# One tower layer of a vision transformer on one core: maxima and exponentials of the next head group issued ahead of the inversion and the splitting of the present one

## The chip, the cores and the metric

The kernel runs on one core of a Trainium2 chip. The metric is the time of one execution on the device in microseconds (us), the median over runs. Five engines run their own instruction streams in order and meet only at semaphores: TensorE (PE, with its weight loads as PEld), VectorE (DVE), ScalarE (ACT), GpSimd (POOL) and SyncE (SP), which here issues every DMA.

## The reference, cut to what matters

For 64 blocks of 128 tokens by 1024 features (the blocks are the filters that a state-space kernel generator makes of the input x), a layer of attention and then one of a feed-forward matrix with low-rank experts are computed:

```python
h = tok(log_dt, x, B, inv_A_real, A_imag, 1024)          # [64, 128, 1024]
h = h + attn(layernorm(h), wq, wk, wv, wo)               # 32 heads of 32, 8 key heads, rotary, causal softmax
h = h + ffn(layernorm(h), W_base, b_base, lora_A, lora_B, router_W, router_b, prior, active)
```

In `attn`, q, k and v are products with 1024 columns of wq and 256 each of wk and wv; scores are masked causally (with 128 tokens the selection of chunks allows every causal position), softmax runs along the keys, and `out @ wo.T` ends it. `ffn` is `x @ W_base.T + b_base` plus four experts of rank 8 weighted by a softmax of the router's logits.

## The kernel before

All products run in float16 in three terms (high by high, high by low, low by high), so each float32 tile that feeds TensorE is first split: ScalarE writes the high half, and another engine the difference, the low half.

The state-space part runs first. Then comes the tower, one **turn** for each block, software-pipelined over four blocks. In turn b, attention's softmax belongs to block b; the q, k and v products (`qkv`) to block n = b+1; the first normalisation (`norm`) to block m+1 = b+3 by its loads and m = b+2 by its statistics; the attention output and the wo product (`rest`) to block p = b-1; and the feed-forward part (`finish`) to block f = b-2. Turns -1 to 3 and 60 to 65 are written out, turns 4 to 59 are a hardware loop of two turns per pass. Each engine's order within a turn is written by hand; nothing reorders it.

The softmax is done in eight groups u = 0 to 7 of four heads. For one group, in order of dependence:

- `scores(u)`, TensorE, L1598: four matmuls into a PSUM buffer (two buffers; it waits for the maxima of group u-2).
- `maxima(u)`, VectorE, L1368 and L1370: masks and scales, writes `probs[u % 4]` and the row maxima. It waits for the scores.
- `exps(u)`, ScalarE, L1227: four exponentials in place, each with its row sum. It waits for the maxima.
- `invert(u)`, VectorE, L1379 and L1381: scales and inverts the sums. It waits for the exponentials.
- `normalise(u)`, GpSimd, L1144: multiplies in place. It waits for the inverted sums.
- `probs_high(u)`, ScalarE, L1236, then `probs_low(u)`, GpSimd, L1148: the split into `p_hl[u % 2]`.
- `turn_probs(u)`, SyncE, L1051: a transposing DMA into `probs_t[u]`, read in the next turn by `attend` (L1620; groups 0 to 3, then 4 to 7).

Around it, on the engines' queues: on TensorE the dense products L1631, `kv` and `q` (they read `xt`), the router product, `ffn(0)`, `ffn(1)`, `wo(0)`, `wo(1)`, and between the first two and the other six groups of three matmuls of `wo(0)` the transpose L1739, which waits for `zs`. `wo(0)` writes a PSUM bank that `add_ffn(0)` must have read. On GpSimd the addition of the bias to `r` (L1194), for which `add_ffn(0)` (L1452) waits; the low half of the normalised input (`low`, L1163), and `rope(2)` (L1154). On VectorE `heads_low` (L1424), `add_ffn(0)`, the router's chain that ends in `zs` (L1531 to L1544), `rope(2)`, `add_ffn(1)`, `add_wo` (L1444) and `add_lora` (L1459). On SyncE, in this order in the second half of a turn: `turn_probs` of groups 3 and 4, then the transpose of the normalised input into `xt` (L1112), then `turn_heads` of part 2, then `turn_probs` of groups 5 and 6. The next turn's `kv` is TensorE's second piece of work in that turn, right behind `scores(0)`, and waits for `xt`.

Of the kernel before, what the change touches and what calls it, by code (L numbers as in the profile page):

```python
# [864 lines left out]
def tower(nc, sem, tok_h, keep, w, ring_of, token_programs, out):  # L865
# [5 lines left out]
    with ExitStack() as ctx:  # L871
# [155 lines left out]
        def _(sp):  # L1027
# [14 lines left out]

            def turn(b, par, attention, qkv, norm, rest, finish):
                n, m, p, f = b + 1, b + 2, b - 1, b - 2

                def turn_probs(c, u):
                    sp.wait_ge(s_plo, c * 8 + (u + 1))
                    await_(sp, s_pv, c * 2 - (1 - u // 4))
                    if not some(c) and isinstance(c, int):
                        sp.wait_ge(prep.wt, prep.jb + u + 2)  # L1050
                    sp.dma_start_transpose(probs_t[:, u].rearrange("p a g t -> p (a g) t"),  # L1051
                                           p_hl[:, u % 2].rearrange("p a g t -> p (a g t)")).then_inc(s_pt[u % 2], 16)

                def turn_heads(of, c):

                    sp.wait_ge(s_hlo, of * 5 + MADE[c])
                    src = heads[:, BLOCK[c]].rearrange("p h t -> p (h t)")
                    if c == "k":
                        await_(sp, s_score, b * 8)
                        dst = kstack[:, 1 - par]  # L1060
                    elif c == 3:
                        await_(sp, s_score, b * 8)
                        dst = stack[:, c]
                    else:
                        if attention:
                            sp.wait_ge(s_score, b * 8 + (2 * c + 2))
                        dst = stack[:, c]
                    sp.dma_start_transpose(dst, src).then_inc(s_st[c], 16)

                if rest:  # L1070

                    await_(sp, s_out, (p - 1) * 16)
                    if not some(p):
                        sp.wait_ge(prep.wt, prep.jend)
                    sp.dma_start(r[:, 1 - par], tok_h[bass.ds(p, 1)].rearrange("o t k -> (o t) k")).then_inc(s_res, 16)
                if attention:
                    turn_heads(b, 3)
                if attention and not some(b):
                    prep.row_out(sp, 3, 5)
                if rest:  # L1080
                    turn_probs(p, 7)
                if finish:
                    sp.wait_ge(s_ylo, f + 1)
                    await_(sp, s_ff, f * 2)
                    sp.dma_start_transpose(yt[:, :, :, :].rearrange("p a c t -> p (a c) t"),
                                           xy_hl[:, :, :].rearrange("p a k -> p (a k)")).then_inc(s_yt, 16)
                if qkv:
                    turn_heads(n, "k")
                if attention:
                    turn_probs(b, 0)  # L1090
                if attention and not some(b):
                    prep.row_in(sp, 3)
                if attention:
                    turn_probs(b, 1)
                    turn_probs(b, 2)
                if norm and (not isinstance(b, int) or m + 1 < CB):
                    sp.wait_ge(s_xhi, m + 1)
                    load_h(m + 1)
                if qkv:
                    turn_heads(n, 0)  # L1100
                    turn_heads(n, 1)
                if qkv and not attention:
                    prep.row_out(sp, 2, 4)
                if attention:
                    turn_probs(b, 3)
                    turn_probs(b, 4)
                if norm:
                    sp.wait_ge(s_xlo, m + 1)
                    if not qkv:
                        sp.wait_ge(prep.ps, 2)  # L1110
                    await_(sp, s_q, n * 2 + 2 if qkv else 0)
                    sp.dma_start_transpose(xt[:, :, :, :].rearrange("p a c t -> p (a c) t"),  # L1112
                                           xy_hl[:, :, :].rearrange("p a k -> p (a k)")).then_inc(s_xt, 16)
                if qkv and not attention:
                    prep.row_in(sp, 2)
                if qkv:
                    turn_heads(n, 2)
                if attention:
                    turn_probs(b, 5)
                    turn_probs(b, 6)  # L1120
                if finish:
                    sp.wait_ge(s_lev, f * 2 + 2)
                    sp.dma_start(out[bass.ds(f, 1)].rearrange("o t k -> (o t) k"), r[:, par]).then_inc(s_out, 16)
# [10 lines left out]
        def _(pool):  # L1134
# [2 lines left out]

            def turn(b, par, attention, qkv, norm, rest, finish):
                n, m, p, f = b + 1, b + 2, b - 1, b - 2

                def normalise(c, u):
                    pool.wait_ge(s_rec, c * 8 + (u + 1))
# [3 lines left out]
                def probs_low(c, u):  # L1146
                    pool.wait_ge(s_phi, c * 8 + (u + 1))
                    TT(p_hl[:, u % 2, 1], probs[:, u % 4], p_hl[:, u % 2, 0], ALU.subtract).then_inc(s_plo, 1)  # L1148
# [32 lines left out]
                if attention:  # L1181
                    probs_low(b, 1)
                    normalise(b, 2)
                    probs_low(b, 2)
                if norm:
                    pool.wait_ge(s_bn1, m * 4 + 4)
                    scale_shift(mean1, var1, rstd1, shift1, s_rstd1, m)
                if attention:
                    normalise(b, 3)
                if finish:  # L1190
                    pool.wait_ge(s_yhi, f + 1)
                    if not some(f):
                        pool.wait_ge(prep.bias, 16)
                    TT(r[:, par], r[:, par], keep["bias"][:, :], ALU.add).then_inc(s_bias, 1)  # L1194
                if attention:
                    probs_low(b, 3)
                    normalise(b, 4)
                    probs_low(b, 4)
                if norm:
                    low(s_xhi, m + 1, s_xlo)  # L1200
                if qkv:
                    rope(2)
                if attention:
                    normalise(b, 5)
                    probs_low(b, 5)
                    normalise(b, 6)
                    probs_low(b, 6)

            at(turn, -2)
            turns(pool, turn)  # L1210

        @block.scalar
        def _(act):
# [2 lines left out]

            def turn(b, par, attention, qkv, norm, rest, finish):
                n, m, p, f = b + 1, b + 2, b - 1, b - 2

                def exps(u):  # L1220

# [74 lines left out]
                if qkv:  # L1296
                    heads_high(0)
                    heads_high(1)
                if attention:
                    probs_high(b, 2)  # L1300
                    exps(3)
                early(3)
                if norm:
                    act.wait_ge(s_rstd1, m * 2 + 2)
# [6 lines left out]
                if finish:  # L1311

                    act.wait_ge(s_lmax, f + 1)
                    A(lexp[:, :], logit[:, :], ACT.Exp, bias=lmax[:, 0:1], scale=1.0, accum_out=lsum[:, 0:1]).then_inc(s_lexp, 1)
                if attention:
                    probs_high(b, 3)
                    exps(4)
                early(4)
                if attention:
                    probs_high(b, 4)  # L1320
                    exps(5)
                early(5)
                if finish:
                    act.wait_ge(s_zt, f + 1)
# [3 lines left out]
                if qkv:  # L1328
                    heads_high(2)
                if attention:  # L1330
                    probs_high(b, 5)
                    exps(6)
                early(6)
                early("last")
                if qkv:
                    heads_high(3)
                if attention:
                    probs_high(b, 6)
                    exps(7)
                early(7)  # L1340

            at(turn, -2)
# [4 lines left out]
        def _(dve):  # L1347
# [9 lines left out]

            def turn(b, par, attention, qkv, norm, rest, finish):
                n, m, p, f = b + 1, b + 2, b - 1, b - 2

                def maxima(u):

# [131 lines left out]
                    attention_low(1)  # L1494

                if attention:
                    invert(b, 2)
                    early(2)
                    maxima(3)
                if qkv:  # L1500
                    v_low()
                if norm:
# [9 lines left out]
                    V.tensor_reduce(lmax[:, :], logit[:, :], AX_X, ALU.max, negate=True).then_inc(s_lmax, 1)  # L1512

                if attention:
                    invert(b, 3)
                    early(3)
                    maxima(4)
                if qkv:
                    heads_low(n, 0)
                    heads_low(n, 1)  # L1520
# [1 line left out]
                    add_ffn(0)  # L1522

                if attention:
                    invert(b, 4)
                    early(4)
                    maxima(5)
                if finish:

                    dve.wait_ge(s_lexp, f + 1)  # L1530
# [18 lines left out]
                    add_ffn(1)  # L1549

                if attention:
                    invert(b, 5)
                    early(5)
                    maxima(6)
                if qkv:
                    heads_low(n, 2)
                early("end")
# [2 lines left out]
                    half_stats(r[:, 1 - par], 0, stats2, s_bn2)  # L1560

                if attention:
                    invert(b, 6)
                    early(6)
                    maxima(7)
                    early(7)
                if finish:
                    add_lora(0)
# [9 lines left out]
        def _(pe):  # L1578
# [2 lines left out]

            def turn(b, par, attention, qkv, norm, rest, finish):
                n, m, p, f = b + 1, b + 2, b - 1, b - 2

                def scores(u):

# [243 lines left out]
```

## Time and profile before

| | |
|---|---|
| three runs | 2990.83, 2992.59, 2999.08 us; median 2992.59 us |
| the profiled execution | 2991.8 us, of which the trace's span is 2990.0 us |
| TensorE busy | 2830.3 us, 95% of the span |
| VectorE busy | 2460.8 us, 82% |
| GpSimd busy | 1971.5 us, 66% |
| ScalarE busy | 1894.5 us, 63% |
| TensorE's granted clock, mean | 0.98 of full speed |

The times of the runs are those of the whole execution; 1.8 us of the profiled one lie outside of its span. A matmul's duration in the trace is its latency: matmuls of 512 columns are shown as 0.38 us long and start every 0.215 us, so TensorE's work is best read from starts.

### The profile page before, as it was taken

What the parts mean: (1) busy time and instruction counts of PE and PEld (TensorE: products, weight loads), DVE (VectorE), ACT (ScalarE), POOL (GpSimd) and SP (SyncE); (2) the same over time, 40 slices, a digit from 0 to 9 for tenths busy, and PEclk for the clock granted to TensorE, in tenths of its full rate; (3) what the DMA queues carried; (4) which work ended last, traced back from release to release, by engine and by line L of the source; (5) the groups of instructions that cost most, each with busy time, mean ns of one, the idle gap of its engine ahead of it and who ended that gap; (6) DMA issues with size and microseconds to landing.
All of it is one profiled execution on the core that took longest, in us unless ns stands there. A gap on an engine that the chain in (4) does not pass through costs nothing.

```text
span 2990.0 us, 62012 instructions
## 1 busy us (share of the span) xinstructions
PE 2830.3 (95%) x16986; PEld 1404.1 (47%) x16986; DVE 2460.8 (82%) x8697; ACT 1894.5 (63%) x5933; POOL 1971.5 (66%) x1734
## 2 busy tenths in 40 slices
PE   4786799999999999999999999999999999999986
PEld 3664444444444444444444444444444444444432
DVE  8997788888888888888888888888888888888872
ACT  5885666666666666666666666666666666666651
POOL 3541577677776677676777766776767777667762
PEclk9997899999999999999999999999999999999988
DMA  8976577666666666666666666666666666666751
GB/s 198 228 212 144 108 143 151 147 148 146 148 146 152 147 143 151 148 148 150 145 149 146 145 154 148 144 148 149 146 152 147 142 149 148 150 147 147 144 117 53
DMA packets 1254159, 442.92 MB, mean 148 GB/s; under 512 B 1200944, under 2 KB 1210032, under 8 KB 1253952
## 3 DMA queue, kind: packets, MB, share of 16 engines
q1 hardware_dynamic: 1253952, 441.02, 65.9%
q14 instruction: 182, 1.49, 0.2%
q8 instruction: 25, 0.41, 0.1%
HBM read 88.55 MB, written 67.11 MB: 52 GB/s over the span
## 4 chain that ended last, share of the span: by engine, by line
PE 58%; DVE 15%; issue 9%; POOL 7%; ACT 6%; DMA 4%; SPq 0%; DVEq 0%; ACTq 0%; POOLq 0%
PE bank_b L1631 29%; PE bank_a L1631 16%; PE bank_c L1631 6%; ACT probs L1227 3%; DVE heads L1424 3%; DVE probs L1370 3%; PE score L1598 3%; POOL p_hl L1148 2%; POOL probs L1144 2%; PE pv L1620 2%; DMA tok_h<-kout 2%; DVE share L1379 1%; POOL rope_a L1154 1%; DMA maxima_rows<-mx 1%; PE kps L490 1%
## 5 line engine op out<-in xcount | busy, mean ns | idle before, releaser
L1227 ACT ACTIVATE probs<-probs,negmax 128x128 f32<-128x128 f32 x2048 | 789.8, 387 | 261.3 <-DVE negmax L1370 261.3
L1148 POOL TENSOR_TENSOR p_hl<-probs,p_hl 128x512 f16<-128x512 f32 x512 | 616.1, 1203 | 344.7 <-ACT p_hl L1236 342.3
L1144 POOL TENSOR_TENSOR probs<-probs,rsum 128x512 f32<-128x512 f32 x512 | 557.6, 1089 | 219.2 <-DVE rsum L1381 218.4
L1631 PE MATMUL bank_a<-qkv_hi,xt 128*128 128x512 f16 x2048 | 652.6, 380 | 1.8 <-DMA xt<-xy_hl 1.8
L1631 PE MATMUL bank_b<-b_hi,yt 128*128 128x512 f16 x2048 | 644.1, 381 | 0.0
L1370 DVE CUSTOM_DVE_ANT_0 probs<-score,table,scal 128x128 f32<-128x128 f32 x2048 | 595.9, 347 | 43.9 <-issue 43.1
L1236 ACT ACTIVATE p_hl<-probs 128x512 f16<-128x512 f32 x512 | 319.9, 625 | 420.1 <-POOL probs L1144 408.7
L1424 DVE TENSOR_TENSOR heads<-rope_a,heads 128x512 f16<-128x512 f32 x320 | 399.0, 1262 | 28.4 <-ACT heads L1257 28.4
L1631 PE MATMUL bank_b<-b_lo,yt 128*128 128x512 f16 x1024 | 390.4, 381 | 0.0
L1631 PE MATMUL bank_a<-qkv_lo,xt 128*128 128x512 f16 x1024 | 389.3, 380 | 0.0
L1631 PE MATMUL bank_b<-o_hi,at_hi 128*128 128x512 f16 x1024 | 388.1, 379 | 0.0
L1631 PE MATMUL bank_b<-o_lo,at_hi 128*128 128x512 f16 x1024 | 388.1, 379 | 0.0
L1631 PE MATMUL bank_b<-o_hi,at_lo 128*128 128x512 f16 x1024 | 388.1, 379 | 0.0
L1227 ACT ACTIVATION_READ_ACCUMULATOR probs<-probs,negmax 128x1 f32 x2048 | 382.9, 187 | 0.0
L1257 ACT ACTIVATE heads<-rope_a 128x512 f16<-128x512 f32 x320 | 192.7, 621 | 229.6 <-POOL rope_a L1154 229.6
L1631 PE MATMUL bank_c<-qkv_hi,xt 128*128 128x512 f16 x1024 | 325.9, 380 | 0.0
L1631 PEld LDWEIGHTS bank_a<-qkv_hi,xt 128*128 128x128 f16 x2048 | 200.8, 98 | 241.6 <-issue 28.9
L1631 PEld LDWEIGHTS bank_b<-b_hi,yt 128*128 128x128 f16 x2048 | 201.0, 98 | 222.7 <-issue 5.4
L1163 POOL TENSOR_TENSOR xy_hl<-xyn,xy_hl 128x1024 f16<-128x1024 f32 x128 | 273.0, 2133 | 30.9 <-ACT xyn L1274 26.0
L1379 DVE TENSOR_TENSOR share<-sums,small 128x4 f32<-128x4 f32 x512 | 197.5, 386 | 61.8 <-ACT probs L1227 61.8
L1154 POOL TENSOR_TENSOR rope_a<-rope_a,rope_b 128x512 f32<-128x512 f32 (+1 forms) x192 | 209.1, 1089 | 55.3 <-DVE rope_b L1407 52.6
L1157 POOL TENSOR_TENSOR rstd<-var,minus_half 128x1 f32<-128x1 f32 x128 | 71.0, 554 | 216.4 <-DVE var L1436 216.3
(202 smaller groups left out, 4573.8 us busy)
## 6 DMA issues: line engine op xcount, KB each, us to landing
tok_h<-kout SPq DMA_DIRECT2D x64, 512.0 KB, 6.1
hin<-tok_h SPq DMA_DIRECT2D x64, 512.0 KB, 3.3
r<-tok_h SPq DMA_DIRECT2D x64, 512.0 KB, 3.8
out_dram<-r SPq DMA_DIRECT2D x64, 512.0 KB, 2.9
probs_t<-p_hl SPq DMA_TRANSPOSE x512, 3.1
xc<-in_x_dram SPq DMA_DIRECT2D x32, 128.0 KB, 4.2
raw_a<-in_L_attn_wq_dram SPq DMA_DIRECT2D x1, 4096.0 KB, 14.3
raw_b<-in_L_attn_wo_dram SPq DMA_DIRECT2D x32, 128.0 KB, 3.6
```

The source lines that it names most:

```text
L1144: TT(x, x, rsum[:, u % 4].unsqueeze(2).to_broadcast([P, GR, T]), ALU.mult).then_inc(s_norm, 1)
L1148: TT(p_hl[:, u % 2, 1], probs[:, u % 4], p_hl[:, u % 2, 0], ALU.subtract).then_inc(s_plo, 1)
L1154: TT(rope_a[:, 0:hs], rope_a[:, 0:hs], rope_b[:, 0:hs], ALU.add).then_inc(s_rope2, 1)
L1163: TT(xy_hl[:, 1], xyn[:, :], xy_hl[:, 0], ALU.subtract).then_inc(done, 1)
L1227: ins = A(probs[:, u % 4, g], probs[:, u % 4, g], ACT.Exp, bias=negmax[:, u % 4, g:g + 1], scale=-1.0, accum_out=sums[:, u % 4, g:g + 1])
L1236: A(p_hl[:, u % 2, 0], probs[:, u % 4], ACT.Copy).then_inc(s_phi, 1)
L1257: A(dst, src, ACT.Copy).then_inc(s_hhi, 1)
L1370: ins = V.tensor_tensor_reduce(probs[:, u % 4, g], score[u % 2][:, g], mask, col(U_SC), 3e38, ALU.add, ALU.min, negmax[:, u % 4, g:g + 1])
L1379: TT(share[:, u % 4], sums[:, u % 4], small[:, :], ALU.mult).then_inc(s_share, 1)
L1424: TT(dst, full_.unsqueeze(2).to_broadcast([P, 8, 2, HD]), hi, ALU.subtract).then_inc(s_hlo, 1)
L1598: ins = MM(score[u % 2][:, g], stack[:, h // 8, h % 8], kstack[:, par, u], start=True, stop=True)
L1631: ins = MM(bank, x(c), w[:, c, cols], start=(c == 0 and i == 0), stop=(c == KC - 1 and i == 2))
```

## The change

In every turn that has attention, on three engines:

- VectorE: `maxima(u+1)` is issued ahead of `invert(u)` for u = 2 to 6 (behind it before).
- ScalarE: `exps(u+1)` is issued ahead of `probs_high(u)` for u = 2 to 6.
- GpSimd: `normalise(3)` comes ahead of `probs_low(2)`, and this one ahead of the bias addition; `normalise(4)` ahead of `probs_low(3)`; `probs_low(4)`, which stood ahead of the low half of the normalised input and of `rope(2)`, now comes behind both and behind `normalise(5)`; `normalise(6)` ahead of `probs_low(5)`.

The orders of TensorE and SyncE stay. No instruction is added or removed (the new name `ahead` is read nowhere). The diff, cut to its core:

```diff
@@ gpsimd
                 if attention:
                     probs_low(b, 1)
                     normalise(b, 2)
-                    probs_low(b, 2)
                 if norm:
                     pool.wait_ge(s_bn1, m * 4 + 4)
                     scale_shift(mean1, var1, rstd1, shift1, s_rstd1, m)
                 if attention:
                     normalise(b, 3)
+                    probs_low(b, 2)
                 if finish:
...
                     TT(r[:, par], r[:, par], keep["bias"][:, :], ALU.add).then_inc(s_bias, 1)
                 if attention:
+                    normalise(b, 4)
                     probs_low(b, 3)
-                    normalise(b, 4)
-                    probs_low(b, 4)
                 if norm:
                     low(s_xhi, m + 1, s_xlo)
                 if qkv:
                     rope(2)
                 if attention:
                     normalise(b, 5)
+                    probs_low(b, 4)
+                    normalise(b, 6)
                     probs_low(b, 5)
-                    normalise(b, 6)
                     probs_low(b, 6)
@@ scalar (the same for 3 and 4, 4 and 5, 5 and 6, 6 and 7)
                 if attention:
+                    exps(3)
                     probs_high(b, 2)
-                    exps(3)
@@ vector (the same for 3 and 4, 4 and 5, 5 and 6, 6 and 7)
                 if attention:
+                    maxima(3)
                     invert(b, 2)
                     early(2)
-                    maxima(3)
```

## Rows read from the trace of the kernel before

**Rows 1.** The page, parts 1 and 2: busy times, and TensorE's clock by slice.

```profile
PE 2830.3 (95%) x16986; PEld 1404.1 (47%) x16986; DVE 2460.8 (82%) x8697; ACT 1894.5 (63%) x5933; POOL 1971.5 (66%) x1734
...
PEclk9997899999999999999999999999999999999988
```

**Rows 2.** Chain that ended last, two turns: start, us, what.

```profile
2806.28 0.65 PE bank_a L1631 x3
...
2847.15 0.65 PE bank_a L1631 x3
```

**Rows 3.** Timeline of TensorE, one turn: start, us, engine, line, operation.

```profile
1510.47 0.39 PE L1598 MATMUL score<-kstack,stack 128*128 128x128 f16 x4
...
1518.68 0.38 PE L1631 MATMUL bank_b<-o_hi,at_hi 128*128 128x512 f16 x1
...
1519.98 0.22 PE L1739 MATMUL pv<-id,zs 128*128 128x128 f16 x1
...
1530.20 0.38 PE L1631 MATMUL bank_a<-qkv_hi,xt 128*128 128x512 f16 x1
```

**Rows 4.** Waits of TensorE's weight loads, 460 to 2830 us: total, times, longest.

```profile
PEld pv L1739 <- DVE zs L1544: 25.1, 56, 1.5
```

**Rows 5.** Timeline of VectorE, the same turn.

```profile
1510.90 0.35 DVE L1370 CUSTOM_DVE_ANT_0 probs<-score,table,scal 128x128 f32<-128x128 f32 x1 [0.70 <-issue]
...
1511.98 3.77 DVE L1424 TENSOR_TENSOR heads<-rope_a,heads 128x512 f16<-128x512 f32 x2
1515.68 0.74 DVE L1452 SCALAR_TENSOR_TENSOR r<-bank_b,scal,r 128x512 f32<-128x512 f32 x1
1516.34 0.15 DVE L1379 TENSOR_TENSOR share<-sums,small 128x4 f32<-128x4 f32 x1
...
1516.72 0.06 DVE L1368 MEMSET marks<- 128x1 f32 x1
...
1517.85 0.16 DVE L1531 RECIPROCAL lrec<-lsum 128x1 f32<-128x1 f32 x1
...
1518.72 1.15 DVE L1544 TENSOR_TENSOR zs<-za,zs 128x64 f16<-128x64 f32 x1
```

**Rows 6.** Timeline of GpSimd, the same turn.

```profile
1511.27 2.37 POOL L1194 TENSOR_TENSOR r<-r,bias 128x1024 f32<-128x1024 f32 x1
1513.68 1.53 POOL L1148 TENSOR_TENSOR p_hl<-probs,p_hl 128x512 f16<-128x512 f32 x1
1516.78 1.04 POOL L1144 TENSOR_TENSOR probs<-probs,rsum 128x512 f32<-128x512 f32 x1 [1.57 <-DVE rsum L1381]
1518.64 1.16 POOL L1148 TENSOR_TENSOR p_hl<-probs,p_hl 128x512 f16<-128x512 f32 x1 [0.82 <-ACT p_hl L1236]
1519.75 2.14 POOL L1163 TENSOR_TENSOR xy_hl<-xyn,xy_hl 128x1024 f16<-128x1024 f32 x1
1521.84 1.27 POOL L1154 TENSOR_TENSOR rope_a<-rope_a,rope_b 128x512 f32<-128x512 f32 x1
```

**Rows 7.** Line L1424 over the span: duration in ns, min, median, max.

```profile
L1424 DVE TENSOR_TENSOR heads<-rope_a,heads x320: 658/882/2849, 276.2 to 2886.4; 128x512 f16<-128x512 f32 x160
```

**Rows 8.** Chain that ended last, the same turn: a group's exponentials.

```profile
1508.15 1.64 ACT probs L1227 x8
```

**Rows 9.** SyncE: line L1051 over the span (min, median, max ns), and an issue.

```profile
L1051 SPq DMA_TRANSPOSE probs_t<-p_hl x512: 1231/1233/2290, 317.4 to 2929.5; - x171
...
1521.92 1.56 SPq L1112 DMA_TRANSPOSE xt<-xy_hl  x1
```

**Rows 10.** DMA issues, 500 to 2800 us: median us from issue to landing.

```profile
xt<-xy_hl SPq DMA_TRANSPOSE x56, 3.6
```

**Rows 11.** Timeline of TensorE in an opening turn.

```profile
378.00 0.48 PE L1631 MATMUL bank_a<-qkv_hi,xt 128*128 128x512 f16 x1 [1.79 <-DMA xt<-xy_hl]
```

**Rows 12.** Stretches around that start: busy us (x count) by engine, PEclk, DMA.

```profile
375.00:380.00 5.00, 2.71 (x12) 0.97 (x11) 4.09 (x19) 3.32 (x11) 3.47 (x4) 0.82 0.86 161
380.00:385.00 5.00, 5.00 (x24) 2.19 (x22) 4.49 (x26) 3.12 (x14) 3.15 (x5) 0.84 0.64 118
```

More of the change, by code:

```diff
@@ L1044, in turn @@
                 n, m, p, f = b + 1, b + 2, b - 1, b - 2
+                ahead = attention
                 def turn_probs(c, u):
@@ L1139, in turn @@
                 n, m, p, f = b + 1, b + 2, b - 1, b - 2
+                ahead = attention
                 def normalise(c, u):
@@ L1218, in turn @@
                 n, m, p, f = b + 1, b + 2, b - 1, b - 2
+                ahead = attention
                 def exps(u):
@@ L1315, in turn @@
                 if attention:
+                    exps(4)
                     probs_high(b, 3)
-                    exps(4)
                 early(4)
                 if attention:
+                    exps(5)
                     probs_high(b, 4)
-                    exps(5)
                 early(5)
@@ L1330, in turn @@
                 if attention:
+                    exps(6)
                     probs_high(b, 5)
-                    exps(6)
                 early(6)
@@ L1337, in turn @@
                 if attention:
+                    exps(7)
                     probs_high(b, 6)
-                    exps(7)
                 early(7)
@@ L1359, in turn @@
                 n, m, p, f = b + 1, b + 2, b - 1, b - 2
+                ahead = attention
                 def maxima(u):
@@ L1514, in turn @@
                 if attention:
+                    maxima(4)
                     invert(b, 3)
                     early(3)
-                    maxima(4)
                 if qkv:
@@ L1524, in turn @@
                 if attention:
+                    maxima(5)
                     invert(b, 4)
                     early(4)
-                    maxima(5)
                 if finish:
@@ L1551, in turn @@
                 if attention:
+                    maxima(6)
                     invert(b, 5)
                     early(5)
-                    maxima(6)
                 if qkv:
@@ L1562, in turn @@
                 if attention:
+                    maxima(7)
                     invert(b, 6)
                     early(6)
-                    maxima(7)
                     early(7)
@@ L1583, in turn @@
                 n, m, p, f = b + 1, b + 2, b - 1, b - 2
+                ahead = attention
                 def scores(u):
```

## The prediction, made before the changed kernel was built

> **What bounds the kernel now.** I read the page first. TensorE is busy 95% of the span and its clock is full in all slices but the opening and the close [rows 1]. Busy time alone says little for pipelined matmuls, so I went to the chain of waits. In the main part it is TensorE without a hole: the last piece of kv starts at 2806.28 in one turn and at 2847.15 in the next, 40.87 us later [rows 2]. A turn has 168 dense matmuls of 512 columns at 0.2155 us (three in 0.65 [rows 2]; 36.2 us in all), and attend, scores, router and low-rank products fill the rest. So 40.87 us is the floor of a turn, and no order of the other engines can go below it. From kv of turn 2 at 378.00 [rows 11] to kv of turn 62, at 2842.39 (the second row of [rows 2] less the 4.76 us that 21 matmuls and four scores take), there are 60 turns of 41.07 us on average. All that a perfect order could gain there is 60 x 0.20 = 12 us.
>
> Next I asked what arrives just in time, because the change can only hurt at such places. Two matter. The transpose of zs: its weight load waits in 56 of the turns between 460 and 2830 [rows 4], and in the turn that I followed zs ends at 1518.72 + 1.15 = 1519.87 [rows 5] while TensorE takes it at 1519.98 [rows 3]. It has no slack at all. And xt: SyncE issues it at 1521.92 [rows 9], it lands 3.6 us later [rows 10], at 1525.5, and kv wants it at 1530.20 [rows 3]: 4.7 us of slack.
>
> **The change part by part.** No work goes or comes, so each term is a shift of a start. I follow the turn around 1510 us with TensorE's starts as they were, and let each engine go on when its queue and its data allow.
>
> *Maxima ahead of inversions.* For u = 2 the cost is hidden: maxima(3) has to wait for the scores, the inversion comes some 1.5 us later, and GpSimd's scale and shift, which wait for VectorE's statistics, set the next start anyway. For u = 3 it isn't. scores(4) start at 1510.47 [rows 3], maxima(4) at 1510.90, and VectorE is free at 1511.98 [rows 5]. Only now comes invert(3), 0.38 us long (1516.34 to 1516.72), so normalise(3) can start at 1512.42 (0.06 us behind the inversion, as at 1516.78 [rows 5, 6]). Before, it stood ahead of the bias addition of 1511.27 [rows 6], so it had ended by then. It is late by over 2 us.
>
> *GpSimd up to the bias.* normalise(3) takes 1.04 us, probs_low(2), newly in front of the bias, 1.16, the bias 2.37, each starting 0.05 us ahead of the last one's end [rows 6]. To this come collisions. The two heads_low operations stand behind maxima(4) on VectorE. Before, they needed 3.77 us together [rows 5], although one alone needs 0.66 at least [rows 7], and the probs_low beside them took 1.53 us in place of 1.16 [rows 6]: they and GpSimd's operations take turns. I charge GpSimd 0.5 us for the first (it starts 0.06 us ahead of normalise(3) and holds it off for most of its length) and 0.4 us for the second, the 0.37 of that row. The bias ends at 1512.42 + 1.04 + 0.5 + 1.11 + 0.4 + 2.33 = 1517.8. Bound: without any collision 1516.9. In the Trainium skill, "SBUF — State Buffer", section "Who interferes with whom", a VectorE instruction with two SBUF inputs and a GpSimd one that reads SBUF exclude each other for the whole instruction; 3.77 us for the two agree. Read as taking no turns at all, it would give the 0.9 us just charged; a reading without a lock would give none of it.
>
> *add_ffn(0) and what is behind it.* It waits for the bias: 1517.9, where it started at 1515.68 [rows 5]. Behind it in VectorE's queue stand maxima(5), invert(4) and the router's chain to zs. By the starts of [rows 5]: add_ffn 0.66, maxima 1.13, inversion 0.38, router steps 0.87, so zs starts at 1521.0. The exponentials of group 4 (1.64 us a group [rows 8]) have long been done, since exps(4) now starts right behind maxima(4) and the second normalised half. normalise(4) starts on GpSimd at 1520.2 and runs to 1521.2; zs, which before ended 0.07 us behind the probs_low that ran beside it (1518.64 + 1.16 [rows 6]), again waits for it: end 1521.3. TensorE takes the transpose at 1521.4 in place of 1519.98: **1.4 us late in every turn**. wo(0) at 1518.68 [rows 3] waits for add_ffn(0), some 0.1 us, within those 1.4.
>
> *xt.* SyncE's order is unchanged: turn_probs(4), then xt. But probs_low(4) has moved behind the low half of the input, rope(2) and normalise(5). GpSimd runs through from 1520.2: normalise(4) 1.00, probs_low(3) 1.11, low half 2.09, rope 1.23, normalise(5) 1.00 (invert(5) is ready by 1524.8, since maxima(6) started at 1523.2), then 0.5 of collision with heads_low of part 2, which waits for rope(2) through ScalarE, and probs_low(4) 1.16: end 1528.3. The issue of turn_probs(4) takes 1.23 us [rows 9] and some 0.1 to the next before xt can be issued, at 1529.7 where it was 1521.92. Landing at +3.6: 1533.3. kv, behind a transpose that is late by 1.4, could have started at 1531.6. It starts at 1533.3: **1.7 us more**. So xt, which had 4.7 us of slack, is 7.8 us later and becomes the wait that ends last.
>
> *The rest.* The last groups gain or lose nothing that counts: probs_low(6) ends near 1533.6, GpSimd needs to be free for the second normalisation's scale at about 1534.1; probs_t of group 7 lands some 0.4 us later against its own start, but attend(1) by then is 1.7 us later too. ScalarE's exponentials come up to 1.2 us earlier, and wait: nobody behind them is the bound. Exponentials of the next group ahead of probs_high(u) cost nothing either, as normalise(u) is later than they are.
>
> *The sum.* A turn is now a loop: kv at 1489.33 (1530.20 - 40.87), scores(4) 21.14 later (TensorE's own pace), and from there the chain over maxima(4), bias, add_ffn(0), maxima(5), GpSimd, SyncE and xt to the next kv, 22.8 later. 44.0 us in place of 41.07, 2.9 x 60 = 176 us. In turns 62 and 63 there is no xt, but the late zs, 1.4 each: 3 us. Turns 0 and 1 have no bias and aren't at TensorE's floor; there exponentials beside normalisation could save 3 us in a turn and the later xt could cost as much: 0, give or take 5. Against the profiled execution, 2991.8 + 179 = 3171 us. The median of the runs is 0.8 above that execution, so 3172.
>
> **The rivals.**
>
> *The clock comes down as well.* TensorE now stands still 1.4 and 1.7 us in each turn. At 378.00 it had waited 1.79 us for xt [rows 11], and the clock was granted at 0.82 and 0.84 in the next two stretches of 5 us, part of them at the lower of its two levels (1.2 GHz against 2.4), in which 0.18 x 5 + 0.16 x 5 = 1.7 us were lost [rows 12]. This lies between kv and scores(4), on the loop. In every turn: 60 x 1.7 = 102 more, 3274. In a third of them: 3206. Against it: this is a single gap, in an opening in which TensorE was less busy all along than it would be in the loop. 2 in 10 for a third of the turns or more.
>
> *Only zs is late.* If xt keeps up (GpSimd quicker than in my walk by over 1.7 us: no collisions, the idle time ahead of normalise(4) shorter), the turn is 41.0 + 1.4 = 42.4: 60 x 1.3 + 3 = 81, so 3074. Without collisions alone, 0.9 + 0.5, the turn would be 42.6: 3087. 1.5 in 10 for this end.
>
> *The other side: TensorE covers it all, and the ends gain.* The one mechanism: with maxima and exponentials ahead, the opening and closing turns that aren't at the floor are shortened, by up to the 1.64 us of exponentials for three groups in turns 0, 1 and 63, 3 us each, so 2984. It decides only if the bias ends before 1515.6, that is if normalise(3) doesn't wait for maxima(4), and xt is issued before 1526.6. The queues as written say the contrary. 0.3 in 10.
>
> *Nothing moves,* because the steady turn hides the shifts: 2992.6. The missing slack of zs [rows 4, 5] speaks against it. 0.4 in 10.
>
> **How the numbers follow.** The walk, 44.0 us a turn within 0.5 (3142 to 3202): 5.5 in 10, the clock 2, zs alone or little more 1.5, no change 0.4, faster 0.3; what is left, 0.3, is a longer loop than any of these. The time is 3172. The range reaches to both neighbours: from 3080, just above zs alone and near the collision-free walk, to 3240, the clock down in two turns of three. Of two executions of this kernel a difference under 0.3% (9 us) can't be told from none. Slower 0.93, the same 0.04, faster 0.03.
>
> **What would show it.** In the profile of the changed kernel: turns of 44 us in TensorE's starts; a wait of TensorE for zs of 1.4 us, and one of kv for the xt transfer of 1.7, in each turn of the loop; bias ending 7.3 us after scores(4); xt issued 40.4 us after kv started, right behind turn_probs(4), which waits for probs_low(4). Wrong would be: xt landing ahead of scores(0) (then the walk on GpSimd is too slow), a clock below 1.00 in the middle slices (then the rival adds), or turns of 41 us.

## The result and the profile after

The changed kernel takes 3243.9 us (3239.6 to 3248.3, 4 runs) against 2993.6 us: 1.084 times the time before, 95% interval 1.082 to 1.085. The direction was right, the loss was larger than forecast: 252 us between the two profiled executions (3243.5 and 2991.8 us) where the walk gave 179, and the time lies 4 us above the stated range.

The page of the changed kernel, busy times and clock by slice (compare [rows 1]):

```profile
PE 2888.3 (89%) x16986; PEld 1409.9 (43%) x16986; DVE 2337.0 (72%) x8697; ACT 1895.1 (58%) x5933; POOL 2015.8 (62%) x1734
...
PEclk9997899999999999999999999999999999999988
```

The work is the same and every engine's share of the span is smaller than before (GpSimd's 62% where it was 66%): somebody waits. The clock's digits are those of the kernel before, but a 9 stands for 90% or more; the mean granted clock is 0.97 where it was 0.98, and the experiments come back to that. Waits of TensorE in the loop, 430 to 3090 us (total, times, longest); in the kernel before its matmuls waited 2.6 us in all between 460 and 2830:

```profile
PE pv L1744 <- DVE zs L1548: 126.7, 59, 2.2
PE bank_a L1636 <- DMA xt<-xy_hl: 56.3, 45, 2.1
PE pv L1625 <- DMA probs_t<-p_hl: 0.6, 1, 0.6
```

These are the two arrivals of the prediction, one in every turn and one in three of four. One turn on TensorE's timeline, cut to five starts (beside [rows 3]): kv, scores(4), wo(0), the transpose of zs, the next kv.

```profile
1515.14 0.38 PE L1636 MATMUL bank_a<-qkv_hi,xt 128*128 128x512 f16 x1 [1.08 <-DMA xt<-xy_hl]
...
1536.39 0.39 PE L1603 MATMUL score<-kstack,stack 128*128 128x128 f16 x4
...
1544.66 0.38 PE L1636 MATMUL bank_b<-o_hi,at_hi 128*128 128x512 f16 x1
...
1548.27 0.23 PE L1744 MATMUL pv<-id,zs 128*128 128x128 f16 x1 [2.15 <-DVE zs L1548]
...
1560.44 0.38 PE L1636 MATMUL bank_a<-qkv_hi,xt 128*128 128x512 f16 x1 [1.75 <-DMA xt<-xy_hl]
```

The turn is 45.30 us long. VectorE in it (beside [rows 5]): maxima(4), add_ffn(0) after 3.43 us of waiting for the bias, and the last steps to zs.

```profile
1536.83 0.35 DVE L1374 CUSTOM_DVE_ANT_0 probs<-score,table,scal 128x128 f32<-128x128 f32 x1 [1.46 <-issue]
...
1538.20 2.14 DVE L1428 TENSOR_TENSOR heads<-rope_a,heads 128x512 f16<-128x512 f32 x2
1543.77 0.75 DVE L1456 SCALAR_TENSOR_TENSOR r<-bank_b,scal,r 128x512 f32<-128x512 f32 x1 [3.43 <-POOL r L1196]
...
1545.98 1.06 DVE L1537 TENSOR_SCALAR alpha<-lexp,lrec 128x4 f32<-128x4 f32 x1
...
1547.50 0.71 DVE L1548 TENSOR_TENSOR zs<-za,zs 128x64 f16<-128x64 f32 x1
```

GpSimd (beside [rows 6]): normalise(3), probs_low(2), bias, normalise(4), probs_low(3), the low half, rope(2), normalise(5), probs_low(4).

```profile
1538.36 1.43 POOL L1146 TENSOR_TENSOR probs<-probs,rsum 128x512 f32<-128x512 f32 x1 [2.42 <-DVE rsum L1385]
1539.75 1.60 POOL L1150 TENSOR_TENSOR p_hl<-probs,p_hl 128x512 f16<-128x512 f32 x1
1541.31 2.34 POOL L1196 TENSOR_TENSOR r<-r,bias 128x1024 f32<-128x1024 f32 x1
1545.98 1.04 POOL L1146 TENSOR_TENSOR probs<-probs,rsum 128x512 f32<-128x512 f32 x1 [2.33 <-DVE rsum L1385]
1546.97 1.15 POOL L1150 TENSOR_TENSOR p_hl<-probs,p_hl 128x512 f16<-128x512 f32 x1
1548.09 2.14 POOL L1165 TENSOR_TENSOR xy_hl<-xyn,xy_hl 128x1024 f16<-128x1024 f32 x1
1550.17 1.28 POOL L1156 TENSOR_TENSOR rope_a<-rope_a,rope_b 128x512 f32<-128x512 f32 x1
1551.76 1.04 POOL L1146 TENSOR_TENSOR probs<-probs,rsum 128x512 f32<-128x512 f32 x1 [0.31 <-DVE rsum L1385]
1552.76 1.61 POOL L1150 TENSOR_TENSOR p_hl<-probs,p_hl 128x512 f16<-128x512 f32 x1
```

SyncE (beside [rows 9]), and xt's time from issue to landing over the span:

```profile
1548.15 7.48 SPq L1052 DMA_TRANSPOSE probs_t<-p_hl  x2
1555.72 1.68 SPq L1113 DMA_TRANSPOSE xt<-xy_hl  x1
...
DMA to landing us min/median/max: 3.7/4.0/10.3
```

The chain is a relay. scores(4) start at 1536.39. VectorE is then busy with maxima(4), so normalise(3) starts at 1538.36; the bias is done at 1543.65, add_ffn(0) starts at 1543.77 and normalise(4) at 1545.98. From there GpSimd works almost without a pause until 1554.37, the end of probs_low(4). The issue of turn_probs(4) closes SyncE's stretch of 7.48 us; xt is issued at 1555.72, 40.58 us after kv, and the next kv starts 4.72 us after that. Over the 60 turns from kv of turn 2 (386.88) to kv of turn 62 (3091.69) a turn takes 45.08 us where it took 41.07.

### The profile page after: what moved, and what is told of

Read it like the earlier page. It is cut to its first block, busy times and chain, and to the rows that moved or that the text cites. A ratio compares the mean times of both kernels' runs of the same rounds, so it can differ in the third digit from the quotient of the medians.

```text
span 3241.7 us, 62012 instructions
## 1 busy us (share of the span) xinstructions
PE 2888.3 (89%) x16986; PEld 1409.9 (43%) x16986; DVE 2337.0 (72%) x8697; ACT 1895.1 (58%) x5933; POOL 2015.8 (62%) x1734
## 4 chain that ended last, share of the span: by engine, by line
POOL 33%; issue 25%; PE 19%; DVE 14%; DMA 5%; ACT 3%; SPq 1%; POOLq 1%; DVEq 0%; ACTq 0%
POOL p_hl L1150 11%; POOL probs L1146 9%; PE bank_b L1636 8%; PE bank_a L1636 7%; POOL r L1196 4%; POOL xy_hl L1165 4%; DVE probs L1374 3%; POOL rope_a L1156 3%; DMA xt<-xy_hl 2%; POOL rstd L1159 1%; PE kps L490 1%; DMA tok_h<-kout 1%; DVE r L1448 1%; DVE alpha L1537 1%; DVE share L1383 1%
## 5 line engine op out<-in xcount | busy, mean ns | idle before, releaser
L1146 POOL TENSOR_TENSOR probs<-probs,rsum 128x512 f32<-128x512 f32 x512 | 581.1, 1135 | 594.3 <-DVE rsum L1385 594.3
L1150 POOL TENSOR_TENSOR p_hl<-probs,p_hl 128x512 f16<-128x512 f32 x512 | 644.6, 1262 | 131.4 <-ACT p_hl L1239 131.1
L1636 PE MATMUL bank_b<-o_lo,at_hi 128*128 128x512 f16 x1024 | 403.4, 394 | 0.0
L1636 PE MATMUL bank_b<-o_hi,at_hi 128*128 128x512 f16 x1024 | 403.4, 394 | 0.0
L1636 PE MATMUL bank_b<-o_hi,at_lo 128*128 128x512 f16 x1024 | 402.9, 393 | 0.0
L1428 DVE TENSOR_TENSOR heads<-rope_a,heads 128x512 f16<-128x512 f32 x320 | 313.9, 998 | 30.1 <-ACT heads L1260 30.1
L1456 DVE SCALAR_TENSOR_TENSOR r<-bank_b,scal,r 128x512 f32<-128x512 f32 x128 | 95.2, 744 | 232.7 <-POOL r L1196 214.1
```

Source lines behind the costliest of these rows:

```text
L1146: TT(x, x, rsum[:, u % 4].unsqueeze(2).to_broadcast([P, GR, T]), ALU.mult).then_inc(s_norm, 1)
L1428: TT(dst, full_.unsqueeze(2).to_broadcast([P, 8, 2, HD]), hi, ALU.subtract).then_inc(s_hlo, 1)
L1636: ins = MM(bank, x(c), w[:, c, cols], start=(c == 0 and i == 0), stop=(c == KC - 1 and i == 2))
```

## The experiments

The ratio of each is to the kernel before, run on the same chip; differences between two experiments are of medians that can come from different chips. Times of a turn are read from TensorE's starts of kv, as above.

**Which engine's order does it.** Three runs: GpSimd's new order alone, VectorE's and ScalarE's new order together, and (at the end of this section) ScalarE's alone. VectorE's alone was not run. The other engines keep the order of before; the first, in short:

```diff
@@ gpsimd: as in the change
@@ scalar, vector: as in the kernel before
```

> Only GpSimd's queue has the new order; VectorE and ScalarE stand as in the kernel before. Theory (two late arrivals: zs, made late by inversions behind maxima and by probs_low(2) ahead of the bias; xt, made late by probs_low(4) behind three operations and by turn_probs(4) ahead of xt on SyncE): normalise(3) is back at its old time, the bias ends about 1.2 us later than before, zs is no longer late, and xt is issued some 4.5 to 5 us later than before, about at the edge of its 4.7 us of slack. A turn of 41 to 42 us, 2990 to 3060 us in all. Rival (GpSimd's order alone carries the loss, the order of VectorE and ScalarE is innocent): a turn of 44 us or more, above 3170 us.

Measured: 3115.0 us, 1.041 (1.039 to 1.042). xt is issued 38.2 to 38.5 us after kv, and zs comes 31.8 to 32.1 us after it, where TensorE would take it at 30.65. So I missed here: zs stays late by 1.2 to 1.5 us even with normalise(3) at its old time. Part of this is that alpha (the router's weights, two steps ahead of zs) now runs beside probs_low(3) and takes 0.92 us where it took 0.23, and zs beside the low half, 1.68 us where it took 1.15; it ends with GpSimd's 2.12 us operation. VectorE in one turn:

```profile
1536.61 0.92 DVE L1535 TENSOR_SCALAR alpha<-lexp,lrec 128x4 f32<-128x4 f32 x1
...
1537.98 1.68 DVE L1546 TENSOR_TENSOR zs<-za,zs 128x64 f16<-128x64 f32 x1
```

The rival's 44 us a turn isn't reached either (43.0).

> Only VectorE's and ScalarE's queues have the new order; GpSimd stands as before. Theory: normalise(3) is 2.2 us late because invert(3) is behind maxima(4), the bias ends about 2.6 us later than before, zs comes 1.0 to 1.5 us late in each turn; xt, issued near 2.5 us later than before, doesn't hold kv up. A turn of 42.0 to 42.6 us, 3050 to 3090 us in all; if TensorE's clock drops behind each wait for zs, up to 1.7 us a turn more, 3190. Rival (the loss needs GpSimd's new order): within 10 us of the kernel before.

Measured: 3104.2 us, 1.037 (1.035 to 1.039), a turn of 42.8 us. Turn and time are above the forecast. In the loop TensorE waits for two things, 0.6 us a turn for zs and about 1 us for something else:

```profile
PE pv L1624 <- DMA probs_t<-p_hl: 58.9, 56, 1.5
PE pv L1743 <- DVE zs L1547: 36.2, 59, 0.6
```

attend(1) waits for the probs of group 7. In the loop of the kernel before they landed 1.1 to 1.7 us ahead of it, and I had counted on xt's lateness to cover a delay of this third arrival; without that it shows.

**Is it xt's place behind turn_probs(4)?**

```diff
@@ sync, changed kernel
                     turn_probs(b, 3)
-                    turn_probs(b, 4)
                 if norm:
                     ...
                     sp.dma_start_transpose(xt[...], xy_hl[...]).then_inc(s_xt, 16)
+                if attention:
+                    turn_probs(b, 4)
```

> The changed kernel with one move on SyncE: the transfer to xt is issued ahead of turn_probs(4). Theory (xt behind turn_probs(4) sets the turn): xt is issued about 36 us after kv in place of 40.5, kv no longer waits, and its time to landing falls to 3.6 us where no probs transfer stands just ahead of it. zs stays late at 33.0 us after kv, 2.4 us behind TensorE, so a turn is 33.0 + 10.3 = 43.3 us: 60 x 1.7 = 104 us less than the changed kernel, 3140. If the drop of TensorE's clock behind the wait for zs, 1.7 us where it occurs, comes in most turns, it is no longer covered by the wait for xt: 44.5 to 45.0 us a turn, 3210 to 3240. Rival (xt is late for what GpSimd does before it, not for its place on SyncE): no change, 3244.

Measured: 3204.5 us, 1.070 (1.068 to 1.072). xt is issued 35.0 us after kv and kv never waits for it in the loop. Of the turns 19 are 43.3 us long, as forecast, ten 44.0 to 44.2, and nearly all others 44.9 to 45.6. Two things add to the forecast. In 18 turns attend(1) waits for the probs of group 7, 11.1 us in all. The larger is the clock behind the wait for zs. Two stretches of this kernel, each beginning about where that wait ends (columns: PE, PEld, DVE, ACT, POOL busy, PEclk, DMA share, GB/s):

```profile
1490.00:1495.00 5.00, 4.81 (x26) 2.36 (x27) 4.50 (x17) 1.87 (x7) 4.69 (x5) 1.00 0.72 153
...
1400.00:1405.00 5.00, 4.68 (x18) 2.02 (x19) 4.50 (x17) 1.75 (x7) 4.69 (x5) 0.66 0.82 171
```

The granted clock is 1.00 in one and 0.66 in the other, most of the latter at the lower level (1.2 GHz), with 18 matmuls in place of 26. The time from zs to the next kv is 10.3 us in one half of the turns and 11.8 to 11.9 in the other (31 of 60): 1.66 us for a wait of 2.15.

The changed kernel has this too, in 23 of its 60 turns. Two of its turns, from the end of the wait for zs, which is 2.15 us long in both:

```profile
1458.00:1463.00 5.00, 4.99 (x19) 2.13 (x20) 4.50 (x16) 2.06 (x9) 4.69 (x4) 0.66 0.47 82
...
1548.25:1553.25 5.00, 4.98 (x27) 2.48 (x28) 4.50 (x16) 2.04 (x9) 4.69 (x4) 1.00 0.39 59
```

There it mostly eats into the wait for xt. In 10 of the 23 turns xt still lands last. In the other 13 kv doesn't wait and starts 11.9 us after zs, which is 0.4 us later than xt would have allowed: 5 us in all. The two costs cover each other, so the removal of xt's 1 us a turn brought 0.7.

**The opening.**

```diff
@@ gpsimd, scalar, vector, changed kernel
+            def turn(b, *rest_):
+                (turn_old if isinstance(b, int) and b in (0, 1) else turn_new)(b, *rest_)
```

> The changed kernel, with turns 0 and 1 in the order of before on all three engines. Theory (the new order also lengthens the two opening turns, which my prediction took as even: kv of turn 2 starts at 386.9 where it was 378.0): kv of turn 2 back at 378 to 379, 8 to 9 us less in all, 3235. Rival (the opening is late for another reason, such as the layout of the program or the first turns' weight preparation): no change, 3244.

Measured: 3239.5 us, 1.082 (1.080 to 1.084), 4.4 us less than the changed kernel; the intervals of the two ratios overlap, so the times alone don't show a gain. In the trace kv of turn 2 starts at 382.97, half of the way back from 386.88. But kv of turn 0, which the change doesn't reach, starts later here than in either kernel (304.44; 302.59 with the change, 302.12 before), and over the traces of all runs it lies between 300.1 and 305.9. Counted from it, turns 0 and 1 take 75.9 us before, 84.3 with the change and 78.5 here. So 8.4 of the 8.9 us arise in turns 0 and 1, and in this pair of traces their order makes 5.8 of them. Where the other 2.6 come from stays open.

**Is it the bias?** GpSimd idles 2.42 us ahead of normalise(3). The bias fits there.

```diff
@@ gpsimd, changed kernel
                 if norm:
                     ...
                     scale_shift(mean1, var1, rstd1, shift1, s_rstd1, m)
+                if finish:
+                    ...
+                    TT(r[:, par], r[:, par], keep["bias"][:, :], ALU.add).then_inc(s_bias, 1)
                 if attention:
                     normalise(b, 3)
                     probs_low(b, 2)
-                if finish:
-                    ...
```

> The changed kernel with the bias addition moved ahead of normalise(3) on GpSimd, into the 2.4 us in which GpSimd waits there for invert(3). Theory (the bias behind normalise(3) and probs_low(2) makes add_ffn(0), maxima(5), zs and normalise(4) late): add_ffn(0) starts 1.5 to 2.5 us earlier against kv, zs is late by under 0.5 us, xt is issued about 38.3 us after kv in place of 40.5, and still behind turn_probs(4): a turn of 42.2 to 43 us, 3070 to 3120 us in all. Rival (VectorE's order alone holds zs up, the bias is innocent): zs stays at 33 us after kv, no change, 3244.

Measured: 3064.4 us, 1.023 (1.021 to 1.024): 180 us of the loss gone by one move, more than the forecast of 3070 to 3120, as xt is issued 37.6 us after kv and not 38.3. zs is in time in the loop (30.65 us after kv), and xt is nearly all that is left:

```profile
PE bank_a L1636 <- DMA xt<-xy_hl: 57.8, 58, 1.7
```

**Both moves together.**

> The changed kernel with both moves: bias ahead of normalise(3), and xt issued ahead of turn_probs(4). Theory (two late arrivals, zs and xt, are the whole loss): both gone, a turn of 41.0 to 41.5 us, 2990 to 3020 us in all, with the look-ahead order otherwise in place. Rival (a third wait comes up: attend(1) for the probs of group 7, which in the run with xt first already took 0.3 to 0.8 us in some turns): 42 us a turn or more, above 3045.

Measured: 2994.3 us, 1.0002 (0.9993 to 1.0011). The look-ahead order with the bias early and xt first costs nothing: a turn is 40.9 us, the floor, in 48 of 60. The third arrival is there, but rarely (7 waits in the loop, 6.3 us).

**A late zs alone,** in the kernel before:

```diff
@@ vector, kernel before
+                if qkv:
+                    rope(2)
                 if finish:
                     dve.wait_ge(s_lexp, f + 1)
                     V.reciprocal(lrec[:, :], lsum[:, :]).then_inc(s_zd, 1)
                     ...
-                if qkv:
-                    rope(2)
```

> The kernel before with one move on VectorE: rope(2), 1.95 us, ahead of the router's chain. A price for a late zs by itself, with nothing else of the change. Theory (each us of lateness of zs is a us of the turn): without port collisions zs is 2.0 us late, a turn of 43.0 us, 3112 us; since alpha and zs then run beside the low half of the input (2.14 us) and rope's addition on GpSimd and wait for their ends, 3.2 us late, a turn of 44.2 us, 3185 us. With a drop of TensorE's clock behind the wait, 1.66 us in each turn where it comes, up to 3280. Rival (TensorE has slack somewhere in the turn that takes this up): under 3050.

Measured: 3112.6 us, 1.039 (1.038 to 1.041). zs is 2.0 us late and the turn 42.93 us. So a us of lateness is a us of the turn; my 3.2 us with collisions was too much, since GpSimd's queue let zs go at the end of its low half, before rope's addition. The clock didn't fall behind any of the 57 waits of 1.5 to 1.9 us, where behind waits of 2.15 us it fell in 31 of 60 turns. Turns 2 to 4 had longer waits, of 3.5, 2.0 and 3.0 us; it fell behind the first two.

**The other direction,** zs ahead of invert(4) in the changed kernel:

```diff
@@ vector, changed kernel
                     maxima(5)
-                    invert(b, 4)
-                    early(4)
                 if finish:
                     dve.wait_ge(s_lexp, f + 1)
                     ...
+                if attention:
+                    invert(b, 4)
+                    early(4)
```

> The changed kernel with the router's chain moved ahead of invert(4), behind maxima(5). Theory (of the 2.3 us for which TensorE waits for zs, about 1.0 is VectorE waiting for GpSimd's normalise(4) and probs_low(3) with alpha and zs, and 0.4 the inversion ahead of them): zs meets an idle GpSimd, alpha takes 0.23 us in place of 1.06 and zs 0.22 in place of 0.71, and the transpose comes 31.6 us after kv in place of 33.0. xt though is issued about 1.1 us later, 41.5 us after kv, as normalise(4) waits for the chain; if xt is what sets the turn, 46.1 us a turn, 3300 us in all. Rival (zs sets the turn, xt only covers it): faster than the changed kernel by 1.4 us a turn, 3160.

Measured: 3350.6 us, 1.118 (1.116 to 1.120). The rival falls: xt sets the turn. Beside an idle GpSimd the last steps were as short as said (alpha 0.23 us, zs 0.22). The loss is larger than my 3300: xt is issued 42.8 us after kv, not 41.5 (the profiled execution, of 3373.6 us, is the longest of five). The clock falls again, now behind the wait for xt (3.1 to 4.2 us; behind 50 of the 59 waits), and this is on the loop itself, between kv and scores(4). TensorE's first matmul of kv, and the stretch that follows it:

```profile
1526.25 0.58 PE L1637 MATMUL bank_a<-qkv_hi,xt 128*128 128x512 f16 x1 [4.00 <-DMA xt<-xy_hl]
```

```profile
1526.00:1532.00 6.00, 5.75 (x16) 2.15 (x17) 3.88 (x18) 2.61 (x10) 2.10 (x4) 0.58 0.87 205
```

**The step that the prediction named.**

```diff
@@ vector, changed kernel
                 if attention:
-                    maxima(4)
                     invert(b, 3)
                     early(3)
+                    maxima(4)
```

> The changed kernel with one pair put back on VectorE: invert(3) ahead of maxima(4). Theory (the step named in my prediction: invert(3) behind maxima(4) makes normalise(3), and with it the bias and zs, late by 2 us, of which probs_low(2) ahead of the bias keeps 1.2): the bias ends 1 us or more earlier, zs comes 31.5 to 32.2 us after kv in place of 33.0, xt is issued near 39.3, a turn of 43 to 43.8 us, 3120 to 3170 us in all. Rival (the later pairs, groups 4 to 6, carry the loss): under 0.3 us a turn, above 3220.

Measured: 3084.1 us, 1.030 (1.028 to 1.031): of the 250 us, 160 hang on this one pair. zs isn't late at all, xt is issued at 38.0 in place of 40.5. The forecast was too high by the lateness of zs that I had carried over from the GpSimd run. Here zs ran beside the end of probs_low(3) and took 0.71 us, there beside the low half, 1.68. Of the 89 us that are left, kv's wait for xt is 80 (1.34 us a turn). What each of the four other pairs costs by itself no run shows.

**Versions against the kernel before.**

> The changed kernel with the bias ahead of normalise(3) and xt ahead of turn_probs(4), and turns 0 and 1 in the order of before on all engines. Theory (the look-ahead order costs 4 us in the two opening turns and nothing in the loop once both arrivals are in time): 4 us less than the version with the two moves alone, 2990 us, 4 us under the kernel before, half of what can be told. Rival (what the opening costs is a matter of the start of the tower, which differs from run to run): equal to the kernel before within 2 us.

Measured: 2990.1 us, 0.9981 (0.9972 to 0.9990), 4.2 us under the version with both moves, as forecast. In the traces turns 0 and 1 take 77.1 us together where they took 82.0. SyncE too has its old order in these two turns.

```diff
@@ vector, kernel before
                     invert(b, 4)
                     early(4)
-                    maxima(5)
                 if finish:
                     dve.wait_ge(s_lexp, f + 1)
                     ...
+                if attention:
+                    maxima(5)
```

> The kernel before with one move on VectorE: the router's chain to zs ahead of maxima(5). Theory (zs has no slack in the kernel before and TensorE waits for it in single turns, 2.6 us in the loop and 1.6 in the opening): these waits go, 4 to 7 us less, 2988 us, near what can be told. Rival (maxima(5) now 1.9 us later makes scores(7), or the exponentials of group 5, late): 2994 or more.

Measured: 2982.9 us, 0.9965 (0.9951 to 0.9979): by the medians 12 us under the kernel before on the same chip, by the interval 6 to 15, and the lowest of all. zs now ends 1.3 us ahead of the transpose that reads it. TensorE's matmuls have no wait between 430 and 2830 us, and 58 of 60 turns are 40.9 us long. So the 0.25 us that every second turn of the kernel before had more was the same missing slack of zs.

**ScalarE alone.**

> Only ScalarE's queue has the new order; VectorE and GpSimd stand as in the kernel before. My prediction said that exponentials of the next group ahead of the splitting cost nothing. Theory (that holds: probs_high(u) comes up to 1.5 us later, xt up to 1.5 us later within its 4.7 us of slack, and zs runs alone on VectorE where it met probs_low(4) before, so it comes about 0.9 us earlier and TensorE's rare waits for it go): 2982 to 2995 us, 41 us a turn. Rival (the later splitting, through probs_low and GpSimd's queue, makes an arrival late, so that ScalarE's order carries a part of the loss of the run with VectorE's and ScalarE's order): above 3010 us.

Measured: 3278.8 us, 1.094 (1.092 to 1.095), more than the whole change. The rival holds. TensorE never waits for zs. Waits of GpSimd, ScalarE and TensorE, 1000 to 1400 us:

```profile
POOL p_hl L1148 <- ACT p_hl L1237: 128.9, 57, 5.7
ACT probs L1228 <- DVE negmax L1371: 100.9, 35, 4.7
...
PE pv L1621 <- DMA probs_t<-p_hl: 23.4, 8, 3.4
```

exps(u+1) stands in front of probs_high(u) but waits for maxima(u+1), which VectorE does only after invert(u): a splitting waits 2 to 3 us for a maximum that it doesn't need. At the end of the turn this reaches the probs of group 7. On SyncE the store of the result goes out 5.2 us after kv (0.9 before), the residual load must wait until it has landed, and turn_probs(7) stands behind both:

```profile
1531.93 1.23 SPq L1051 DMA_TRANSPOSE probs_t<-p_hl  x1
1533.22 0.57 SPq L1123 DMA_DIRECT2D out_dram<-r  x1
1536.94 0.32 SPq L1075 DMA_DIRECT2D r<-tok_h  x1
1537.36 1.24 SPq L1068 DMA_TRANSPOSE stack<-heads  x1
1538.70 1.97 SPq L1051 DMA_TRANSPOSE probs_t<-p_hl  x1
```

```profile
1543.10 0.62 PE L1621 MATMUL pv<-probs_t,v_hi 128*32 128x512 f16 x4 [3.26 <-DMA probs_t<-p_hl]
```

```profile
1543.00:1549.00 6.00, 5.90 (x23) 1.99 (x24) 1.96 (x6) 3.21 (x10) 4.93 (x5) 0.51 0.73 153
```

TensorE waits 3.26 us in attend(1) and then works at a granted clock of 0.51, the lower level, for nearly the whole of 6 us. Over the loop, 430 to 3120 us:

```profile
PE pv L1621 <- DMA probs_t<-p_hl: 162.7, 56, 3.4
```

In 51 turns the clock falls behind this wait, and TensorE is at the lower level for 256 us in all. At half speed that loses up to 128 us (an estimate): the waits and the clock together cover the 281 us.

## Why the prediction was right in kind and too small

- *Maxima ahead of inversions, u = 3.* The step was right, and putting the pair back shows it (160 us). normalise(3) started 1.97 us after scores(4), in the walk 1.95.
- *Up to the bias.* Right: its end came 7.26 us after scores(4), in the walk 7.3. The two collisions were 0.39 and 0.44 us, charged as 0.5 and 0.4.
- *zs.* The term was mis-sized: 2.3 us late, not 1.4. I had let only the last step wait for GpSimd. alpha waited too, 1.06 us in place of 0.23, and then zs met probs_low(3), 0.71 in place of the 0.22 that it takes beside an idle GpSimd. In the Trainium skill, "SBUF — State Buffer", section "Who interferes with whom", `tensor_scalar` is named among the operations that can enter a mode using both ports and then contend with GpSimd, if their operands allow that mode. alpha is a `tensor_scalar` and its row agrees; which mode it ran in no run here shows. I hadn't applied it.
- *xt.* Its issue was right: 40.4 us after kv forecast, 40.46 in most turns and 40.55 on average. The step that failed is "Landing at +3.6: 1533.3", with kv starting at that same moment. From issue to kv it was 4.5 us on average over the loop, in two parts. xt landed after 4.2 us on average, not 3.6. And kv started 0.3 us behind the landing: 0.23 us in each turn of the hardware loop where kv waited, which the walk had put at nothing, and the rest from the clock. With the 0.15 us of the issue that is 1.1 us in each of 60 turns, most of what was missing: 45.08 against 44.0, 65 us.
- *Why xt lands later.* The row of 3.6 us is of a kernel in which xt is issued 2.1 us behind the previous transfer. There, and with turn_probs(4) moved behind xt (again 2.1 us), it lands after 3.7 us on average. In the changed kernel it is issued 1.3 us behind turn_probs(4); GpSimd alone and bias early have the same distance, with means of 4.3 and 4.2. With both moves it is 1.3 to 1.7 us behind turn_probs(3), mean 4.0. So the distance goes with the landing in all these runs. It isn't the whole cause: in the changed kernel, at the same distance, the landing mostly alternates between 3.9 us in one turn and 4.5 to 4.9 in the next, and why is open.
- *The opening.* Forecast as even, give or take 5; it came 8.9 us later, 8.4 of it in turns 0 and 1. Their order makes 5.8 and 4.9 us in the two pairs of traces, 4.4 and 4.2 in the medians of times; the rest stays open.
- *The close.* From kv of turn 62 to the end of the span it took 150.0 us in place of 147.8, forecast 3 more.
- The sum: 60 x 4.01 + 8.9 + 2.3 = 252 us.
- *The rival of the clock* was half right. The clock does fall, in 23 of 60 turns, more than the third that I had given 2 in 10. But it falls behind the wait for zs, not where I had priced it, between kv and scores(4), and mostly hides under the wait for xt. It added about 5 us that way, and 1.7 in the single turn in which it fell behind kv's wait (2.1 us); I had said 34 for a third of the turns. It is also a reason why removing one of the two waits brings less than that wait (xt first: 39 us, not 104).
- *"Exponentials ahead cost nothing either"* holds in the version with both moves, where the maxima are ahead too. Alone they are the costliest of the parts measured. The losses of the parts aren't additive: 121 for GpSimd, 110 for VectorE with ScalarE, 281 for ScalarE, 250 for all.

## What to carry to other kernels

When the engine that sets the time waits for almost nothing, a reordering elsewhere can hardly gain, and what it loses is read from the few arrivals with least slack: list them with their slack before moving anything (here zs 0.1 us, probs of group 7 1.1 to 1.7, xt 4.7). Work that an urgent arrival hangs on goes where its queue idles: one bias addition moved into a 2.4 us gap and one transfer moved ahead of another gave back the whole 250 us, and 1.3 us of slack for zs made the kernel before 12 us faster. An instruction put ahead that waits for a partner still behind on another engine blocks its whole queue: the exponentials ahead without the maxima cost 281 us, with them 110. And two waits in one turn can cover each other, so the price of one is read only with the other gone.

## What the runs showed of the hardware

- No wait of TensorE under 2 us in the loops read was followed by a lower granted clock (57 waits of 1.5 to 1.9 us for a late zs alone; 59 of kv, 0.9 to 1.8 us, with invert(3) back). Waits of 2.15 us were followed by one in 23 of 60 turns (changed kernel) and in 31 of 60 (xt first), with about 1.7 us lost each time. After waits of 3.1 to 4.2 us the clock fell in 50 of 59 cases (zs ahead of invert(4)). It didn't after one wait of 3.0 us.
- The transposing transfer of a group's probs occupies SyncE for 1.23 us when nothing holds it up, the one to xt for about 1.6. The transfer to xt lands after 3.7 us on average when it is issued 2.1 us behind the transfer before it, and after 4.0 to 4.3 us on average, 4.9 in single turns, when it is 1.3 to 1.7 us.
- A VectorE instruction of 4 elements a partition takes 1.06 us, not 0.23, when a GpSimd one of 1.04 us has just begun, and 0.92 when it has begun 0.27 us before; a subtraction of 128x64 takes 0.22 us alone, and 0.71 or 1.68 beside a GpSimd operation, with which it then ends.
